# Copies of the rows of B and C in a state-space scan: two halves of 64 partitions that carry both, issued by SyncE

## The chip, the cores and the metric

One core of one Trainium2 chip. The time is the device time of one execution in microseconds (us), the median of several runs. The engines are TensorE (PE), VectorE (DVE), ScalarE (ACT), GpSimd (POOL) and SyncE (SP), with 16 DMA engines beside them. TensorE's clock has two levels, 1.2 and 2.4 GHz; the profile gives the granted clock as a mean, 1.00 being 2.4 GHz.

## The reference

Eight sequences of 512 tokens with 128 features go through four residual blocks, each after a layer norm: a state-space block, an FFN of 8 experts (all computed for all tokens, mixed by a softmax), a windowed attention of 16 heads, and the FFN again. The part that the change touches is the scan of the state-space block:

```python
b_term = jnp.tanh(b_raw)                       # [B, L, 8]
c_term = jnp.tanh(c_raw)                       # [B, L, 8]
decay = jnp.clip(jnp.exp(-delta[..., None] * a), 0.0001, 1.0)
drive = (1.0 - decay) * (b_term[:, :, None, :] * xb[..., None])
# over the tokens t, for 64 channels and 8 states:
state = dec_t * state + drv_t
y = jnp.sum(state * c_t[:, None, :], axis=-1) + D * x_t
```

b_term and c_term have one row for each of the 8 states, the same for all 64 channels.

## The kernel before

Features stand on the partitions and the 512 tokens in the free dimension. The time is laid out in chunks. A chunk is 128 of the 4096 hidden units of the FFN for one sequence: three fp32r matmuls of 512 columns for the gate and three for the up projection (weights and inputs are split in a high and a low part), SiLU on ScalarE (L1056), the product with the up projection on VectorE (L1094), and four down projections a little later (L1001). A pass has 32 chunks and there are 16 passes, so 512 chunks. The state-space block and the attention are woven in between: every engine has its own program, made by `interleave` (L938), which merges generators in the order of the slots that they yield. A slot is a time in chunks; it decides only the order of instructions on an engine, and the waits on semaphores decide when they run. The order on one engine is strict: behind a waiting instruction all others of this engine wait.

The scan of sequence i (i from 0 to 7) handles the 8 states in four steps k, two states at a time: partitions 0 to 63 are the 64 channels of state 2k, partitions 64 to 127 those of state 2k + 1. "State k" stands for such a step below. Sequence 0 is done ahead of the FFN with a spreading by TensorE. For sequences 1 to 7 `Ssm.spread` (L596) stores the 16 rows of B and C (`bc_rows`) in DRAM and reads them back spread: the two rows of B of step k, each to 64 partitions, go into `btile`, those of C into `ctile`. Both tiles are double, k % 2, and lie in `arena` at rows 6 and 7 (B) and 8 and 9 (C). The steps of a state, by line:

- ACT L493: exp, gives the decay. Waits for the y product of state k - 2.
- POOL L628: clips the decay. POOL L630: B times x (waits for the B copy).
- DVE L581 and L582: the drive, then the scan over 512 tokens.
- POOL L634: C times the state (waits for the C copy and the scan). POOL L638 adds it to y for k > 0; for k = 0 DVE L587 does.

The copy of B for state k waits for the scan of state k - 2 (L608), that of C for its y (L612). Both are issued by ScalarE, B at slot k - 2 and C at slot k + 0.5. The slots of the four states are 9, 12, 15, 18 for sequence 1 and 36, 39, 42, 45 for sequence 2; for sequences 3 to 7 they are o + 10, o + 16, o + 26, o + 32 with o = 64 (i - 2).

The attention of sequence j begins at slot 38 + 55j. On SP, `Att.sp` (L818) stores q and k to DRAM at +7 (L832), reads them back in another layout at +8 (L838: 8 copies of 256 KB), stores V at +9 (L845), and reads it back in windows at +12 and +20.2 (L860, 2 x 8 copies). POOL then makes masked queries (L883) and masked V (L891). SP also loads the inputs (L920), stores the outputs (L929) and reloads a residual buffer once the store has landed (L932, L933). The store of sequence b is at the end of its second FFN pass, two to four slots ahead of the first B copy of sequence b + 4.

The B copy before:

```python
act.dma_start(btile[k % 2], bc_r[2 * k:2 * k + 2, :].unsqueeze(1)
             .broadcast_to([2, INNER, L])).then_inc(b_moved[k % 2], 16)
```

Of the kernel before, what the change touches and what calls it, by code (L numbers as in the profile page):

```python
# [13 lines left out]
B, L, D = 8, 512, 128  # L14
P = 128
TT = L // P
INNER, DSTATE, DTRANK = 64, 8, 8
# [18 lines left out]
NC = NCH * NM  # L36
# [9 lines left out]
def _ssm_slots(i):  # L46
    if i == 0:
        return dict(ln=-33, win=-31, dt=-26, k=(-24, -23, -22, -21), y=-19)
    if i == 1:
        return dict(ln=1.5, win=3.5, dt=6, k=(9, 12, 15, 18), y=23.5)  # L50
    if i == 2:
        return dict(ln=26, win=28.5, dt=32, k=(36, 39, 42, 45), y=50.5)
    o = NCH * (2 * i - 4)
    return dict(ln=o + -9, win=o + -6.5, dt=o + 1, k=(o + 10, o + 16, o + 26, o + 32), y=o + 42)


T_SSM = [_ssm_slots(i) for i in range(B)]
T_ATT = [38 + 55 * b for b in range(B)]
ATT_PACE = [3.3] + [4.1] * (B - 2) + [3.22]

# [21 lines left out]
def build(nc, x_d, pack_d, wg_d, wu_d, wd_d, out_d):  # L82
    ctx = contextlib.ExitStack()
    with ctx:
# [3 lines left out]
        def sem(name):  # L88
            s = ctx.enter_context(nc.semaphore(name))
            sems.append(s)  # L90
            return s
# [41 lines left out]
        arena = sb("arena", [P, 10, L])  # L133
        xb2, zb, delta, tot, cv, sxT = (arena[:, i, :] for i in range(6))
        btile, ctile = ([arena[:, i + s, :] for s in range(2)] for i in (6, 8))
        bc_t = sb("bc_rows", [2 * DSTATE, L])
# [63 lines left out]
        bc_out = sem("bc_out")  # L200
        silu_x, xs_m, xs_done = sem("silu_x"), sem("xs_m"), sem("xs_done")
        dt_soft, delta_done = sem("dt_soft"), sem("delta_done")
        bx_done, dec_exp, scan_done = sem("bx_done"), sem("dec_exp"), sem("scan_done")
        dec_clip = sem("dec_clip")
        y_part, y_done, b_moved, c_moved = sem("y_part"), sem("y_done"), [sem("b_moved0"), sem("b_moved1")], [sem("c_moved0"), sem("c_moved1")]
        x_hi, qk_hi, qk_moved = sem("x_hi"), sem("qk_hi"), sem("qk_moved")
        qk_out = [[sem(f"{v}_{part}_out") for part in ("hi", "lo")] for v in "qk"]
        v_zero, v_pad, v_out, v_moved, p_t = sem("v_zero"), sem("v_pad"), sem("v_out"), [sem(f"v_moved{i}") for i in range(2)], sem("p_t")
# [57 lines left out]
        b = Banks(side_ps, side_full, side_free)  # L266
# [115 lines left out]
        class Ssm:  # L382
            @staticmethod
            def pe(pe, link, i):
                at = T_SSM[i]
                yield at["ln"]
# [206 lines left out]
                b.wait_free(dve, ("y", i))  # L593

            @staticmethod
            def spread(act, link, i):  # L596

                at = T_SSM[i]
                bc_r = bc_d[i % 2]
                yield at["dt"] + 1  # L600
                b.wait_free(act, ("bc", i))
                act.dma_start(bc_r, bc_t[:, :]).then_inc(bc_out, 16)
                for k in range(KT):
                    n = KT * i + k
                    yield at["k"][k] - 2
                    if k == 0:
                        act.wait_ge(bc_out, 16 * i)
                    act.wait_ge(scan_done, n - 1)  # L608
                    act.dma_start(btile[k % 2], bc_r[2 * k:2 * k + 2, :].unsqueeze(1)
                                 .broadcast_to([2, INNER, L])).then_inc(b_moved[k % 2], 16)  # L610
                    yield at["k"][k] + 0.5
                    act.wait_ge(y_done, n - 1)  # L612
                    act.dma_start(ctile[k % 2], bc_r[DSTATE + 2 * k:DSTATE + 2 * k + 2, :].unsqueeze(1)
                                 .broadcast_to([2, INNER, L])).then_inc(c_moved[k % 2], 16)

            @staticmethod
            def pool(pool, link, i):
                at = T_SSM[i]
                yield at["ln"] - 2
                norm_pool(pool, link, "ssm_ln", i)  # L620
                if i == 0:
                    return
                for k in range(KT):
                    n = KT * (i - 1) + k
                    d, bt, ct = dec[:, k % 2, :], btile[k % 2], ctile[k % 2]
                    yield at["k"][k] + 1.5
                    pool.wait_ge(dec_exp, KT * i + k + 1)
                    nc.gpsimd.tensor_scalar(d, d, 1e-4, 1.0, ALU.max, ALU.min).then_inc(dec_clip, 1)  # L628
                    pool.wait_ge(b_moved[k % 2], 16 * (n // 2 + 1))
                    nc.gpsimd.tensor_tensor(bt, bt, xb2, ALU.mult).then_inc(bx_done, 1)  # L630
                    yield at["k"][k] + 3.5
                    pool.wait_ge(c_moved[k % 2], 16 * (n // 2 + 1))
                    pool.wait_ge(scan_done, KT * i + k + 1)
                    nc.gpsimd.tensor_tensor(ct, ct, d, ALU.mult).then_inc(y_part, 1)  # L634
                    if k:
                        pool.wait_ge(y_part, n + 1)
                        pool.wait_ge(y_done, KT * i + k)
                        nc.gpsimd.tensor_tensor(tot, tot, ct, ALU.add).then_inc(y_done, 1)  # L638
# [299 lines left out]
        def interleave(jobs, eng, link, step):  # L938

            streams = []  # L940
            for program, k in jobs:
                gen = program(eng, link, k)
                streams.append([next(gen), gen])

            def run(c):
                while streams:
                    first = min(streams, key=lambda s: s[0])
                    if first[0] > c:
                        return
                    slot = next(first[1], None)  # L950
                    if slot is None:
                        streams.remove(first)
                    else:
                        first[0] = max(first[0], slot)

            for c in range(-SETUP, NC + LAG + 3):
                for _ in step(c) or ():
                    run(c)
                run(c + 0.5)
            run(10 ** 6)  # L960
# [6 lines left out]
        with nc.Block() as block:  # L967
# [47 lines left out]
            @block.sync  # L1015
            def _(sp):
                sp.dma_start(x_raw[:, :, :], tok(x_d, 0)).then_inc(raw_loaded, 16)
                sp.dma_start(pack[:, :], pack_d[:, NRAW:NPACK]).then_inc(packed, 16)
                sp.dma_start(raw, pack_d[:, 0:NRAW]).then_inc(raw_packed, 16)

                def chunk(c):
                    j = c + SETUP - 1
                    if 0 <= j < 2 * E:
                        if j >= NH:
                            sp.wait_ge(w_lo, j - NH + 1)
                        sp.dma_start(h_b[:, j % NH, :], (wg_d, wu_d)[j // E][j % E]).then_inc(w_loaded[j % NH], 16)
                    e = c + SETUP - 1 - 2 * E
                    if 0 <= e < E:
                        sp.dma_start(wd[:, CPE * e:CPE * (e + 1), :],
                                     wd_d[e].rearrange("(c p) h -> p c h", p=P)).then_inc(wd_loaded, 16)  # L1030

                interleave([(load_x, i) for i in range(B)] + [(store, i) for i in range(B)]
                           + [(pad_v, 0)] + [(Att.sp, j) for j in range(B)], sp, None, chunk)
                sp.wait_ge(stored, 16 * B)

            @block.scalar
            def _(act):
                link = Chain(act, act_step)

                def split_w(j):  # L1040
                    act.wait_ge(w_loaded[j % NH], 16 * (j // NH + 1))
                    nc.scalar.copy(w_part(j, 0), h_b[:, j % NH, :]).then_inc(w_hi, 1)

                def chunk(c):
                    if c < 0:
                        if 0 <= c + SETUP - 8 < 2 * E:
                            split_w(c + SETUP - 8)
                        return
                    if c < NC:
                        act.wait_ge(g_full, c + 1)  # L1050
                        if c == 0:
                            act.wait_ge(w_lo, 2 * E)
                            act.wait_ge(w_small, 2)
                        if c >= NH:
                            act.wait_ge(down_done, c - NH + 1)
                        nc.scalar.activation(h_b[:, c % NH, :], pg[c % 2][:, :], ACT.Silu).then_inc(gate_done, 1)  # L1056
                    yield

                def small_weights(act, link, k):
                    yield -SETUP  # L1060
                    act.wait_ge(w_prep, 1)
                    link(nc.scalar.activation(neg_a[:, :], neg_a[:, :], ACT.Exp, scale=-1.0))
                    nc.scalar.activation(neg_a[:, :], neg_a[:, :], ACT.Ln, bias=1.0).then_inc(w_prep, 1)

                interleave([(small_weights, 0)] + [(Ssm.act, i) for i in range(B)] + [(Ssm.spread, i) for i in range(1, B)] + [(Att.act, j) for j in range(B)]
                           + [(Head.act, m) for m in range(NM)], act, link, chunk)

            @block.vector
# [159 lines left out]
```

## Time and profile before

The runs had 1530.69 to 1531.13 us, median 1531.04. The profiled execution:

| | |
|---|---|
| time of the profiled execution | 1530.76 us |
| span | 1529.0 us |
| PE busy | 1442.1 us, 94% of the span |
| DVE busy | 946.7 us, 62% |
| ACT busy | 772.8 us, 51% |
| POOL busy | 503.1 us, 33% |
| ACT's queue (q10) | 14.91 MB, 2.7% of 16 engines |
| SP's queue (q1) | 58.58 MB, 14.7% of 16 engines |

Busy time of an engine is a sum over its instructions. A row of instructions gives the start, the duration, the engine, the line of the code, output and input by name, and in square brackets how long the engine was idle before it and what ended that. ACTq and SPq are issues of DMAs by the queues of these engines. "DMA share" is the mean busy share of the 16 DMA engines.

### The profile page before, as it was taken

To read this page: it belongs to the slowest core of one execution; us is meant where nothing else is said; L and a number is where in the kernel's file an instruction comes from. 1 tells how busy PE (TensorE), PEld (TensorE's weight loads), DVE (VectorE), ACT (ScalarE), POOL (GpSimd) and SP (SyncE) were. 2 spreads that over 40 slices of the span, in tenths; PEclk is the share of its full clock that TensorE was granted. 3 is DMA by queue.
4 is the path that set the end of the run, shared out by engine and by line. 5 is a ranking of instruction groups with operands and counts; after the bars stand their busy time and mean duration, and the time that the engine had idled before them with its cause. 6 is when DMAs were issued, how large, how long until landed. Compare 5 with 4: busy or idle time off the path is not lost.

```text
span 1529.0 us, 31357 instructions
## 1 busy us (share of the span) xinstructions
PE 1442.1 (94%) x12756; PEld 1247.8 (82%) x12756; DVE 946.7 (62%) x2125; ACT 772.8 (51%) x1037; POOL 503.1 (33%) x446
## 2 busy tenths in 40 slices
PE   5788889999999999999999989999999999999998
PEld 3677767888878878888888778888888888888887
DVE  5645558665766757666676566757765566575543
ACT  6453726654457444654546465455643554355321
POOL 5241344323432354135520373117511421241000
PEclk9999999999999999999999999999999999999999
DMA  5110151004201330024001510042004200420000
GB/s 184 33 48 23 45 143 32 19 27 131 40 2 41 105 81 2 9 89 116 14 2 39 134 43 13 1 136 57 29 2 118 40 2 1 118 40 1 2 7 8
DMA packets 82092, 75.50 MB, mean 49 GB/s; under 512 B 4748, under 2 KB 60076, under 8 KB 81948
## 3 DMA queue, kind: packets, MB, share of 16 engines
q1 hardware_dynamic: 74444, 58.58, 14.7%
q10 hardware_dynamic: 7504, 14.91, 2.7%
q8 instruction: 101, 1.65, 0.4%
q14 instruction: 43, 0.35, 0.1%
HBM read 60.65 MB, written 12.83 MB: 48 GB/s over the span
## 4 chain that ended last, share of the span: by engine, by line
PE 71%; DVE 9%; DMA 6%; ACT 5%; issue 5%; POOL 3%; SPq 1%; ACTq 0%; DVEq 0%; POOLq 0%
PE pd L1001 23%; PE pg L272 7%; PE pu L272 6%; PE pg L274 6%; PE pg L273 6%; PE pu L273 6%; PE pu L274 6%; DMA arena<-bc_spread 3%; PE att_ps L678 3%; DVE h L1094 2%; PE att_ps L700 2%; PE att_ps L705 1%; POOL arena L628 1%; DVE ffn_rows L295 1%; DMA qk_rows<-qk_parts 1%
## 5 line engine op out<-in xcount | busy, mean ns | idle before, releaser
L1056 ACT ACTIVATE h<-pg 128x512 f32<-128x512 f32 x512 | 303.4, 597 | 693.7 <-PE pg L274 687.5
L1001 PEld LDWEIGHTS pd<-w_down,h 128*128 128x128 f32 x4096 | 517.4, 194 | 31.9 <-issue 2.5
L1001 PE MATMUL pd<-w_down,h 128*128 128x128 f32 x4096 | 530.1, 278 | 0.8 <-DVE x L1082 0.8
L1094 DVE TENSOR_TENSOR h<-h,pu 128x512 f32<-128x512 f32 x512 | 345.6, 679 | 222.4 <-PE pu L274 220.7
L272 PE MATMUL pg<-ffn_x_hi,w_gate_hi 128*128 128x512 f32 x512 | 246.3, 481 | 1.5 <-DVE ffn_x_lo L355 1.5
L272 PE MATMUL pu<-ffn_x_hi,w_up_hi 128*128 128x512 f32 x512 | 207.0, 404 | 25.1 <-DVE h L1094 24.7
L273 PE MATMUL pg<-ffn_x_lo,w_gate_hi 128*128 128x512 f32 x512 | 204.6, 400 | 0.0
L274 PE MATMUL pg<-ffn_x_hi,w_gate_lo 128*128 128x512 f32 x512 | 204.4, 399 | 0.0
L273 PE MATMUL pu<-ffn_x_lo,w_up_hi 128*128 128x512 f32 x512 | 204.3, 399 | 0.0
L274 PE MATMUL pu<-ffn_x_hi,w_up_lo 128*128 128x512 f32 x512 | 204.2, 399 | 0.0
L903 POOL TENSOR_TENSOR att_arena<-att_arena 128x512 f32<-128x512 f32 (+1 forms) x72 | 72.8, 1011 | 349.4 <-DVE att_arena L775 349.2
L883 POOL TENSOR_TENSOR q_weights<-q,pack 128x512 fp32r<-128x512 f32 x136 | 140.8, 1056 | 79.9 <-DMA k<-qk_rows 79.9
L1056 ACT ACT_TABLE_LOAD x121 | 155.2, 1283 | 3.7 <-issue 1.6
L1082 DVE SCALAR_TENSOR_TENSOR x<-pd,mix,x 128x128 f32<-128x128 f32 x512 | 143.8, 344 | 20.3 <-PE pd L1001 14.8
L272 PEld LDWEIGHTS pu<-ffn_x_hi,w_up_hi 128*128 128x128 f32 x512 | 97.4, 190 | 57.4 <-DVE h L1094 34.6
L274 PEld LDWEIGHTS pg<-ffn_x_hi,w_gate_lo 128*128 128x128 f32 x512 | 97.7, 191 | 23.8
L274 PEld LDWEIGHTS pu<-ffn_x_hi,w_up_lo 128*128 128x128 f32 x512 | 97.2, 190 | 23.9
L273 PEld LDWEIGHTS pu<-ffn_x_lo,w_up_hi 128*128 128x128 f32 x512 | 97.5, 190 | 22.6
L272 PEld LDWEIGHTS pg<-ffn_x_hi,w_gate_hi 128*128 128x128 f32 x512 | 99.5, 194 | 9.9 <-issue 3.4
L273 PEld LDWEIGHTS pg<-ffn_x_lo,w_gate_hi 128*128 128x128 f32 x512 | 99.6, 195 | 5.0 <-issue 1.7
L628 POOL TENSOR_SCALAR arena<-arena 128x512 f32<-128x512 f32 x28 | 54.4, 1942 | 134.9 <-ACT arena L493 133.9
L733 ACT ACT_TABLE_LOAD x71 | 91.1, 1283 | 1.3
(192 smaller groups left out, 1539.2 us busy)
## 6 DMA issues: line engine op xcount, KB each, us to landing
arena<-bc_spread ACTq DMA_DIRECT2D x56, 256.0 KB
att_arena<-v_rows SPq DMA_DIRECT2D x64, 144.0 KB, 3.9
qk_rows<-qk_parts SPq DMA_DIRECT2D x32, 256.0 KB, 3.1
q<-qk_rows SPq DMA_DIRECT2D x32, 256.0 KB, 3.7
k<-qk_rows SPq DMA_DIRECT2D x32, 256.0 KB, 4.5
att_arena<-v_rows SPq DMA_DIRECT2D x64, 128.0 KB, 3.6
arena<-in_x SPq DMA_DIRECT2D x8, 256.0 KB, 2.8
x<-in_x SPq DMA_DIRECT2D x8, 256.0 KB, 3.5
```

Of the source, the lines that this page charges most:

```text
L272: nc.tensor.matmul(out, w[0], x_parts[0], start=first, stop=False)
L273: nc.tensor.matmul(out, w[0], x_parts[1], start=False, stop=False)
L274: return nc.tensor.matmul(out, w[1], x_parts[0], start=False, stop=last)
L628: nc.gpsimd.tensor_scalar(d, d, 1e-4, 1.0, ALU.max, ALU.min).then_inc(dec_clip, 1)
L678: last = nc.tensor.matmul(ps[:, (4 * i + g) * WK:(4 * i + g + 1) * WK], q_w[:, n % 2, i, g, :, :].rearrange("p r q -> p (r q)"), k3[:, g, ...
L733: nc.scalar.activation(u, u, ACT.Exp, scale=float(HD) ** -0.5).then_inc(s_exp, 1)
L883: nc.gpsimd.tensor_tensor(q_w[:, n % 2, i, :, :, :], q3[:, :, w * WQ:w * WQ + QW].bitcast(F32).unsqueeze(2) .broadcast_to([P, 4, 4, QW]), ...
L903: nc.gpsimd.tensor_tensor(u, u, smax[:, 0:nw, :].unsqueeze(3).broadcast_to([P, nw, 4, WK]), ALU.subtract).then_inc(s_sub, 1)
L1001: last = nc.tensor.matmul(pd[:, t * P:(t + 1) * P], h_b[:, d % NH, t * P:(t + 1) * P], wd[:, d % NCH, :], start=d % CPE == 0 and t == 0, s ...
L1056: nc.scalar.activation(h_b[:, c % NH, :], pg[c % 2][:, :], ACT.Silu).then_inc(gate_done, 1)
L1082: nc.vector.scalar_tensor_tensor(x[:, t, :], pd[:, t * P:(t + 1) * P], mix[m % 2][:, t, e % E:e % E + 1], x[:, t, :], ALU.mult, ALU.add).t ...
L1094: nc.vector.tensor_tensor(h, h, pu[d % 2][:, :], ALU.mult).then_inc(h_done, 1)
```

## The change

One copy carries, for one half h of the partitions, the B row and the C row of state 2k + h: it writes 64 partitions x 2 rows x 512, from two rows of DRAM that lie 8 apart. Two such copies, h = 0 and 1, make a state. They are issued together, by SP instead of ScalarE, at the slot `bc`, and wait for the scan and for the y of state k - 2. The `bc` slot is k - 2 or, where that is later, 5.5 slots behind the slot of state k - 2: 7, 10, 14.5, 17.5 in sequence 1; 34, 37, 41.5, 44.5 in sequence 2; k - 2 from sequence 3 on. The store of the 16 rows moves to SP too. POOL waits for both copies in front of L630 and no longer in front of L634.

```diff
--- before.py
+++ after.py
@@ -55,6 +55,9 @@
 
 
 T_SSM = [_ssm_slots(i) for i in range(B)]
+for t in T_SSM:
+
+    t["bc"] = [max(k - 2, t["k"][n - 2] + 5.5 if n >= 2 else -NC) for n, k in enumerate(t["k"])]
 T_ATT = [38 + 55 * b for b in range(B)]
 ATT_PACE = [3.3] + [4.1] * (B - 2) + [3.22]
 
@@ -202,7 +205,7 @@
         dt_soft, delta_done = sem("dt_soft"), sem("delta_done")
         bx_done, dec_exp, scan_done = sem("bx_done"), sem("dec_exp"), sem("scan_done")
         dec_clip = sem("dec_clip")
-        y_part, y_done, b_moved, c_moved = sem("y_part"), sem("y_done"), [sem("b_moved0"), sem("b_moved1")], [sem("c_moved0"), sem("c_moved1")]
+        y_part, y_done, bc_moved = sem("y_part"), sem("y_done"), [sem("bc_moved0"), sem("bc_moved1")]
         x_hi, qk_hi, qk_moved = sem("x_hi"), sem("qk_hi"), sem("qk_moved")
         qk_out = [[sem(f"{v}_{part}_out") for part in ("hi", "lo")] for v in "qk"]
         v_zero, v_pad, v_out, v_moved, p_t = sem("v_zero"), sem("v_pad"), sem("v_out"), [sem(f"v_moved{i}") for i in range(2)], sem("p_t")
@@ -593,25 +596,25 @@
                 b.wait_free(dve, ("y", i))
 
             @staticmethod
-            def spread(act, link, i):
+            def spread(sp, link, i):
 
                 at = T_SSM[i]
                 bc_r = bc_d[i % 2]
                 yield at["dt"] + 1
-                b.wait_free(act, ("bc", i))
-                act.dma_start(bc_r, bc_t[:, :]).then_inc(bc_out, 16)
+                b.wait_free(sp, ("bc", i))
+                sp.dma_start(bc_r, bc_t[:, :]).then_inc(bc_out, 16)
                 for k in range(KT):
                     n = KT * i + k
-                    yield at["k"][k] - 2
+                    yield at["bc"][k]
                     if k == 0:
-                        act.wait_ge(bc_out, 16 * i)
-                    act.wait_ge(scan_done, n - 1)
-                    act.dma_start(btile[k % 2], bc_r[2 * k:2 * k + 2, :].unsqueeze(1)
-                                 .broadcast_to([2, INNER, L])).then_inc(b_moved[k % 2], 16)
-                    yield at["k"][k] + 0.5
-                    act.wait_ge(y_done, n - 1)
-                    act.dma_start(ctile[k % 2], bc_r[DSTATE + 2 * k:DSTATE + 2 * k + 2, :].unsqueeze(1)
-                                 .broadcast_to([2, INNER, L])).then_inc(c_moved[k % 2], 16)
+                        sp.wait_ge(bc_out, 16 * i)
+                    sp.wait_ge(scan_done, n - 1)
+                    sp.wait_ge(y_done, n - 1)
+
+                    for h in range(2):
+                        sp.dma_start(arena[h * INNER:(h + 1) * INNER, 6 + k % 2:10:2, :],
+                                      bc_r[2 * k + h::DSTATE, :].unsqueeze(0)
+                                      .broadcast_to([INNER, 2, L])).then_inc(bc_moved[k % 2], 16)
 
             @staticmethod
             def pool(pool, link, i):
@@ -626,10 +629,9 @@
                     yield at["k"][k] + 1.5
                     pool.wait_ge(dec_exp, KT * i + k + 1)
                     nc.gpsimd.tensor_scalar(d, d, 1e-4, 1.0, ALU.max, ALU.min).then_inc(dec_clip, 1)
-                    pool.wait_ge(b_moved[k % 2], 16 * (n // 2 + 1))
+                    pool.wait_ge(bc_moved[k % 2], 32 * (n // 2 + 1))
                     nc.gpsimd.tensor_tensor(bt, bt, xb2, ALU.mult).then_inc(bx_done, 1)
                     yield at["k"][k] + 3.5
-                    pool.wait_ge(c_moved[k % 2], 16 * (n // 2 + 1))
                     pool.wait_ge(scan_done, KT * i + k + 1)
                     nc.gpsimd.tensor_tensor(ct, ct, d, ALU.mult).then_inc(y_part, 1)
                     if k:
@@ -1030,7 +1032,7 @@
                                      wd_d[e].rearrange("(c p) h -> p c h", p=P)).then_inc(wd_loaded, 16)
 
                 interleave([(load_x, i) for i in range(B)] + [(store, i) for i in range(B)]
-                           + [(pad_v, 0)] + [(Att.sp, j) for j in range(B)], sp, None, chunk)
+                           + [(pad_v, 0)] + [(Ssm.spread, i) for i in range(1, B)] + [(Att.sp, j) for j in range(B)], sp, None, chunk)
                 sp.wait_ge(stored, 16 * B)
 
             @block.scalar
@@ -1062,7 +1064,7 @@
                     link(nc.scalar.activation(neg_a[:, :], neg_a[:, :], ACT.Exp, scale=-1.0))
                     nc.scalar.activation(neg_a[:, :], neg_a[:, :], ACT.Ln, bias=1.0).then_inc(w_prep, 1)
 
-                interleave([(small_weights, 0)] + [(Ssm.act, i) for i in range(B)] + [(Ssm.spread, i) for i in range(1, B)] + [(Att.act, j) for j in range(B)]
+                interleave([(small_weights, 0)] + [(Ssm.act, i) for i in range(B)] + [(Att.act, j) for j in range(B)]
                            + [(Head.act, m) for m in range(NM)], act, link, chunk)
 
             @block.vector
```

## Rows read from the trace of the kernel before

**Rows 1.** The chain that ended last, by engine, whole span.

```profile
PE 71%; DVE 9%; DMA 6%; ACT 5%; issue 5%; POOL 3%; SPq 1%; ACTq 0%; DVEq 0%; POOLq 0%
```

**Rows 2.** Groups of instructions, 1440 to 1500 us: busy, mean ns, idle before.

```profile
L1056 ACT ACTIVATE h<-pg 128x512 f32<-128x512 f32 x26 | 15.5, 598 | 42.1 <-PE pg L274 42.1
```

**Rows 3.** Windows: length, busy time by engine, granted clock, DMA share, GB/s.

```profile
core 0: us, PE busy (x) PEld busy (x) DVE busy (x) ACT busy (x) POOL busy (x), PEclk, DMA share, GB/s
100.00:110.00 10.00, 8.02 (x41) 6.67 (x40) 4.02 (x8) 5.03 (x6) 5.75 (x4) 0.84 0.13 49
200.00:210.00 10.00, 6.11 (x29) 4.47 (x28) 5.26 (x9) 1.79 (x3) 2.93 (x3) 0.94 0.65 209
850.00:890.00 40.00, 32.19 (x235) 28.16 (x234) 18.18 (x32) 13.48 (x17) 18.72 (x15) 0.83 0.47 109
1030.00:1070.00 40.00, 38.57 (x413) 33.08 (x412) 28.13 (x48) 21.84 (x28) 29.05 (x21) 0.96 0.26 60
```

**Rows 4.** Waits, whole span: total us, times, longest.

```profile
POOL arena L634 <- DMA arena<-bc_spread: 48.0, 11, 7.8
...
POOL arena L630 <- DMA arena<-bc_spread: 9.8, 8, 2.9
```

**Rows 5.** Timeline of POOL, states of sequences 1 and 2.

```profile
81.88 1.93 POOL L628 TENSOR_SCALAR arena<-arena 128x512 f32<-128x512 f32 x1 [25.10 <-ACT arena L493]
84.39 1.29 POOL L630 TENSOR_TENSOR arena<-arena 128x512 f32<-128x512 f32 x1 [0.59 <-DMA arena<-bc_spread]
...
105.79 1.27 POOL L630 TENSOR_TENSOR arena<-arena 128x512 f32<-128x512 f32 x1 [0.72 <-DMA arena<-bc_spread]
111.14 1.27 POOL L634 TENSOR_TENSOR arena<-arena 128x512 f32<-128x512 f32 x1 [4.08 <-DMA arena<-bc_spread]
112.49 1.28 POOL L638 TENSOR_TENSOR arena<-arena 128x512 f32<-128x512 f32 x1
113.85 1.92 POOL L628 TENSOR_SCALAR arena<-arena 128x512 f32<-128x512 f32 x1
116.48 1.26 POOL L630 TENSOR_TENSOR arena<-arena 128x512 f32<-128x512 f32 x1 [0.71 <-DMA arena<-bc_spread]
...
178.49 1.28 POOL L630 TENSOR_TENSOR arena<-arena 128x512 f32<-128x512 f32 x1 [2.01 <-DMA arena<-bc_spread]
```

**Rows 6.** DMA issues, whole span: count, KB each, median us to landing.

```profile
q<-qk_rows SPq DMA_DIRECT2D x32, 256.0 KB, 3.7
...
arena<-in_x SPq DMA_DIRECT2D x8, 256.0 KB, 2.8
```

**Rows 7.** Timeline of VectorE: a scan of sequence 1, then the L581 of sequence 2.

```profile
107.17 0.69 DVE L581 SCALAR_TENSOR_TENSOR arena<-arena 128x512 f32<-128x512 f32 x1 [5.94 <-POOL arena L630]
107.90 1.22 DVE L582 TENSOR_TENSOR_SCAN arena<-arena 128x512 f32<-128x512 f32 x1
...
179.88 0.69 DVE L581 SCALAR_TENSOR_TENSOR arena<-arena 128x512 f32<-128x512 f32 x1 [2.61 <-POOL arena L630]
...
191.24 0.69 DVE L581 SCALAR_TENSOR_TENSOR arena<-arena 128x512 f32<-128x512 f32 x1 [5.62 <-POOL arena L630]
...
204.70 1.66 DVE L581 SCALAR_TENSOR_TENSOR arena<-arena 128x512 f32<-128x512 f32 x1 [4.84 <-POOL arena L630]
```

**Rows 8.** Timeline of ScalarE's queue: the first B copy, and one in sequence 2.

```profile
76.81 1.08 ACTq L609 DMA_DIRECT2D arena<-bc_spread  x1
...
181.87 4.50 ACTq L609 DMA_DIRECT2D arena<-bc_spread  x1
```

**Rows 9.** The chain of waits at sequence 6's states: start, length.

```profile
837.78 7.01 DMA qk_rows<-qk_parts
...
849.33 10.65 DMA k<-qk_rows
```

**Rows 10.** Timeline of POOL in sequence 4's last state and sequence 6's states.

```profile
536.81 2.04 POOL L883 TENSOR_TENSOR q_weights<-q,pack 128x512 fp32r<-128x512 f32 x2 [6.31 <-DMA k<-qk_rows]
...
541.59 1.27 POOL L630 TENSOR_TENSOR arena<-arena 128x512 f32<-128x512 f32 x1 [0.73 <-DMA arena<-bc_spread]
...
860.05 4.03 POOL L883 TENSOR_TENSOR q_weights<-q,pack 128x512 fp32r<-128x512 f32 x4 [3.25 <-DMA k<-qk_rows]
...
877.50 1.89 POOL L891 TENSOR_TENSOR att_arena<-att_arena,pack 128x1024 f32<-128x1024 f32 x1 [9.07 <-DMA att_arena<-v_rows]
```

## The prediction

> **What bounds the kernel now.** Read the engine shares first. TensorE is busy for most of the span and holds most of the chain that ended last; DMA has only 6% of that chain [rows 1]. In the last stretch, where nothing runs beside the FFN, 26 SiLU evictions take 60 us, so a chunk costs 2.31 us [rows 2]: that is TensorE's own pace. What can be gained is the time in which TensorE falls off it, so the next view is the windows. In the stretches where the state updates of sequences 1 and 2 run, PE is busy 8.02 and 6.11 of 10 us at a granted clock of 0.84 and 0.94; where those of sequence 6 run, 32.19 of 40 us at 0.83 [rows 3]. These are the late places, and in each the line of waits leads to the copies of B and C. POOL waited 48.0 us in 11 waits at L634 and 9.8 us in 8 at L630 for them [rows 4]. (A wait goes to what came last, so part of the 4.08 us in front of an L634 is VectorE's scan.)
>
> Why the copies are late is in the window of sequence 1: nothing else moves there, the DMA share is 0.13 and the rate 49 GB/s [rows 3]. 0.13 is 2 of 16 engines (0.125). B and C each write [2, 64, 512]: two state rows, each repeated 64 times, with the 2 outermost. The pace agrees: the multiplications L630 of two consecutive states, each released by its B copy, start at 105.79 and 116.48 [rows 5], and between two B copies lies one C copy, so 512 KB take 10.69 us, 5.35 us a copy.
>
> A rule of the Trainium skill ("DMA: Bandwidth & Descriptors", section "Rules for kernel authors") says that the outermost dimension's size caps the number of DMA engines, a small leading broadcast included. For a before-copy that gives 2, and this trace agrees (0.13); for the new copies, with 64 outermost, it gives 16, which no row here shows for this shape. The sum below needs only that a pair lands within 7 us.
>
> **What the change does.** (a) 56 copies of 256 KB stay 56 copies of 256 KB, but each carries B and C for 64 partitions, 64 outermost. Their landing isn't in the trace of before. Nearest rows: other 256 KB copies whose outermost size is 32 or 128 land in a median of 3.7 us (in a queue of four) and 2.8 us [rows 6]; the old form needs 10.7 us for two. I take 4 us a pair: 2.8 us, plus 0.5 us for the second issue (the issue cost of 0.5 us is that of the old ones, and stays two a state), plus 0.7 us for its bytes (5.35 us x 2 of 16 engines). Ends: 3 us and 10.7 us.
>
> (b) The state chain of sequence 1. A step is L628, L630 on POOL, L581 and L582 on VectorE, L634, L638 on POOL. Its bare length: L628 1.92, L630 1.27, VectorE from 107.17 to 109.12 = 1.95, L634 1.27, L638 1.28, and five hand-overs of about 0.1: 8.2 us [rows 5, 7]. It now runs at 10.69, the pace of the DMA. The slots leave 3 chunks a step, 6.9 us at 2.31, so TensorE stays bound by the chain, through the multiplication L1094 queued behind L581 on VectorE, both before and after. Three steps between the first L581 and the last save 3 x 2.5 = 7.5 us, and the 0.59 us that the first L630 waited [rows 5] go too: **8 us**.
>
> (c) Sequence 2. VectorE was idle 2.61, 5.62 and 4.84 us before the L581 of states 1, 2 and 3 [rows 7], so it was ready at 177.3, 185.6 and 199.9. State 1: L630 at 178.49 had waited 2.01 for B [rows 5], so L581 comes at 177.9, ready and released, instead of 179.88. State 2: one bare step later, 186.1, after VectorE's 185.6, instead of 191.24. State 3: before, VectorE got ready 8.6 us after the L581 of state 2, more than a bare step (8.2): 186.1 + 8.6 = 194.7 instead of 204.70. **10 us.** In this stretch ScalarE's own queue also stood behind an issue of 4.50 us [rows 8]; that stall goes as well, inside the same 10 us.
>
> (d) Sequence 6 collides with the attention of sequence 4, whose q and k go to DRAM and back on all 16 engines, two of which are still full of B and C. The last of four stores lands 7.01 us after issue, the last k copy 10.65 us after its own [rows 9], where the medians were near 3.7 [rows 6]; POOL's queries start only at 860.05 and its first V mask at 877.50 after 9.07 us of wait [rows 10]. PE is idle 7.8 of the 40 us from 850, and a clock of 0.83 means a third of them at the lower level (1.2 instead of 2.4 GHz), 6.8 us of full-speed work: some 13 us in all, where the two overlap a little. Sequence 7's states, 1030 to 1070, have the same work and an attention beside it, and lose 1.4 + 1.6 = 3.0 us [rows 3]. With the copies spread, a pair adds 128 x 2 / 16 = 16 packets to an engine, some 1.4 us, instead of 10.7 us to two. I take **8 us** of the 10 between them.
>
> (e) Sequence 4, state 3: POOL's L883 waited 6.31 us for k and L630 another 0.73 for B [rows 10]. L630 can start about 2.5 us earlier with TensorE idle behind it: **2.5 us**. For sequences 3, 5 and 7 I count nothing: B lands before POOL gets there.
>
> (f) Issues leave ScalarE: 63 at about 0.5 us, 31 us. They lie under table loads and waits for TensorE; worth 0, bound 0 to 3 us. On SP they cost nothing of themselves, but SP runs in order: behind a waiting pair stand the q/k stores (sequence 2: slots 44.5 and 45), the V reads (sequences 5 and 7), and before pair 0 of sequences 4 to 7 the store of a result and the reload that waits for it, some 4 us. The pair is issued 3.5 slots (8 us) before L630 wants it and takes 4, so this is worth 0, bound 0 to -4 us.
>
> (g) The new wait: B now waits for y of the state two before, not only its scan. That is L587 or L638, which end a whole bare step or nearly (8 to 10 us) before L630 wants the pair; 4 us fit. Cost 0, up to a pair of 8 us.
>
> **Sum.** 8 + 10 + 8 + 2.5 = 28.5 us. The profiled execution took 1530.76 us (span 1529.0); less 28.5 is 1502.3, and the median of the runs lies 0.3 higher: 1502.6, say **1503**. Bounds: all of (d) and 3 us of (f), -37 us; or (d) at nothing, (c) at 7 us and (e) at 2, -17 us.
>
> **The rivals.**
> 1. Half comes back. The attention start of sequence 6 is late by POOL's order, not by DMA: between 864 and 884 POOL also has masks, queries and states, and in sequence 2 the q/k/V round trip then ends last. For: at 860.05 stands L883 x4, a POOL job of 4.03 us, before the next L628. Against: each of these jobs is preceded by a DMA wait [rows 10]. Then 8 + 7 + 0 + 2 = 17 us: 1514.
> 2. More than counted: with less idling the clock stays at its upper level, and the sequence 6 stretch comes back whole. 37 us: 1494.
> 3. Slower. The copies stay narrow, on two engines or as slow by reading the same two rows 16 times at once. A pair then takes 10.7 us and POOL can't begin L630 before C is in too, where it now needs B alone: 5.35 us later at state 0 of sequences 1 and 2, the pace of 10.7 unchanged after it. Plus 11 us: 1542. It decides from a pair time of about 7 us (issue 76.81 [rows 8] to the end of L628 at 83.8 [rows 5]). For: every engine would read the same 4 KB, which no row shows. Against: one engine reads one 2 KB row 64 times over now without a visible penalty.
> 4. It does nothing measurable, since TensorE makes up the lateness elsewhere. Against: it can't run faster than 2.31 us a chunk [rows 2], and in most windows it does so already.
>
> One more rule of the Trainium skill speaks against the cut ("SBUF — State Buffer", section "Can I just issue two DMAs to hit both halves?"): a copy of 64 partitions reaches only half of the SBUF's ports, and two such copies run one behind the other. An estimate by its 196 GB/s for 64 partitions is 1.3 us a copy, a pair in about 5 us with a fixed cost of 2; no row here shows a 64-partition copy. By it the sum stays, with 2 us of slack instead of 3, and rival 3 gets nearer.
>
> **Chances.** Forecast 0.60, rival 1 0.22, rival 2 0.08, rival 3 0.06, rival 4 0.04. A difference under 0.2% (3 us) can't be told from none. Faster 0.90, same 0.04, slower 0.06. Range 1492 to 1518: it holds the forecast, rival 2 and rival 1 with its spread.
>
> **What would show it.** In the windows of sequence 1's states the DMA share stands in bursts well over 0.13, and L630 has no DMA wait. The L630 starts of sequence 1 lie 8.2 us apart, not 10.7. The POOL waits on B and C fall from 58 us to under 5. The k copies of sequence 6's time land in under 6 us and queries start before 855. SP shows new waits on L587 or L638, with nothing urgent behind them. Wrong: copies still at 5 us each; a step still over 10 us; or TensorE's idle time moved to another wait of the same length.

## The result and the profile after

The changed kernel takes 1492.66 us (median of 4 runs, 1490.37 to 1494.68) against 1530.87 us: a ratio of 0.9754, 95% interval 0.9739 to 0.9768, 38 us faster. (The 1530.87 us are the median of the runs above with one more, of 1529.60.) The range, from 1492 us, held the median by 0.7 us, and two of the four runs lie below it; the forecast of 1503 us was 10 us too high. Runs in a slower state of the chip (two of the first four of the width-only kernel below, 2548 and 2817 us, and one of the narrow kernel's four, 1627 us) are in none of the times and ratios here. The profiled execution took 1493.85 us, with a span of 1492.1 us.

The chain that ended last (from the page of the profile), by engine, and the DMA row of the new copies: DMA has 1% of it where it had 6% [rows 1].

```profile
PE 77%; DVE 10%; ACT 5%; issue 5%; POOL 4%; DMA 1%; DVEq 0%; SPq 0%; POOLq 0%; ACTq 0%
...
arena<-bc_spread SPq DMA_DIRECT2D x56, 256.0 KB, 4.8
```

The timeline of POOL in sequence 1 (start, duration; L631, L633, L636 and L640 are L628, L630, L634 and L638 of before):

```profile
82.54 1.93 POOL L631 TENSOR_SCALAR arena<-arena 128x512 f32<-128x512 f32 x1 [24.82 <-ACT arena L496]
84.55 1.28 POOL L633 TENSOR_TENSOR arena<-arena 128x512 f32<-128x512 f32 x1
...
100.47 1.28 POOL L633 TENSOR_TENSOR arena<-arena 128x512 f32<-128x512 f32 x1
103.89 1.29 POOL L636 TENSOR_TENSOR arena<-arena 128x512 f32<-128x512 f32 x1 [2.14 <-DVE arena L585]
105.26 1.27 POOL L640 TENSOR_TENSOR arena<-arena 128x512 f32<-128x512 f32 x1
106.62 1.91 POOL L631 TENSOR_SCALAR arena<-arena 128x512 f32<-128x512 f32 x1
108.61 1.27 POOL L633 TENSOR_TENSOR arena<-arena 128x512 f32<-128x512 f32 x1
```

See two things. Two L633 of consecutive states start 8.14 us apart (100.47, 108.61), where it was 10.69 [rows 5]; and no line has a wait for DMA; nor has any POOL instruction a wait for B or C in the whole span, where these waits were 57.8 us [rows 4]. In front of L636 only the scan is left, 2.14 us where 4.08 stood.

Windows, with the columns of [rows 3]: two short ones in sequence 1, and 40 us of sequence 6's states, which now come some 24 us earlier (the window is moved by 22).

```profile
78.00:80.00 2.00, 1.97 (x9) 1.31 (x8) 1.58 (x5) 1.42 (x4) 0.00 (x0) 1.00 0.68 223
...
100.00:110.00 10.00, 9.41 (x58) 7.96 (x57) 4.91 (x10) 5.68 (x7) 7.42 (x6) 1.00 0.19 53
...
828.00:868.00 40.00, 39.02 (x366) 33.88 (x364) 28.83 (x58) 23.98 (x30) 27.96 (x23) 1.00 0.42 83
```

The copies come in bursts (223 GB/s at a DMA share of 0.68, so at least 11 of the 16 engines) instead of a steady 49. PE is busy 9.41 us of the ten (8.02 before), and in sequence 6 39.02 of 40 at a clock of 1.00 (32.19 at 0.83 before, [rows 3]).

Where the time went is read most simply from one instruction that stands in both kernels 512 times, the SiLU of a chunk (L1056 before, L1058 after). Its start in the two profiled executions, from the trace, us:

```
chunk                  0      8     24     40     56    160    168    272    280    344    352    504
before               56.1   78.0  127.5  175.5  232.6  534.1  558.8  856.7  892.1 1073.5 1100.2 1501.2
after                57.0   78.7  119.6  167.8  212.9  514.1  534.9  832.9  856.8 1036.7 1063.3 1464.3
earlier by           -1.0   -0.7    7.9    7.8   19.8   20.0   24.0   23.8   35.4   36.9   36.9   36.9
```

All of it is gained in five short places, and between them the two executions run in step: 8.6 us at sequence 1's states (chunks 8 to 24), 12.0 at sequence 2's (40 to 56), 4.0 at sequence 4's last state (160 to 168), 11.6 where sequence 6 meets attention 4 (272 to 280), 1.5 in sequence 7 (344 to 352). The start is 1 us later. (One execution of each kernel is profiled, so a place is known to about 1 us.)

SP's queue has the new waits for y (L590 and L640 are L587 and L638 of before; waits of the queue: total, times, longest), and behind them nothing that was late: POOL's waits for k fell from 79.9 to 71.3 us in all, and its 9.1 us for V are gone.

```profile
SPq L612 <- DVE arena L590: 86.0, 5, 32.5
...
SPq L612 <- POOL arena L640: 33.3, 4, 13.6
```

### The profile page after: what moved, and what is told of

The parts are those of the page before. It is cut to its first block, busy times and chain, and to the rows that moved or that the text cites. A ratio compares the mean times of both kernels' runs of the same rounds, so it can differ in the third digit from the quotient of the medians.

```text
span 1492.1 us, 31350 instructions
## 1 busy us (share of the span) xinstructions
PE 1427.2 (96%) x12756; PEld 1236.2 (83%) x12756; DVE 950.3 (64%) x2125; ACT 773.0 (52%) x1037; POOL 504.3 (34%) x446
## 4 chain that ended last, share of the span: by engine, by line
PE 77%; DVE 10%; ACT 5%; issue 5%; POOL 4%; DMA 1%; DVEq 0%; SPq 0%; POOLq 0%; ACTq 0%
PE pd L1003 25%; PE pg L275 7%; PE pu L275 7%; PE pg L277 6%; PE pu L276 6%; PE pg L276 6%; PE pu L277 6%; PE att_ps L680 3%; DVE h L1096 2%; PE att_ps L702 2%; POOL arena L631 1%; PE att_ps L707 1%; DVE ffn_rows L298 1%; POOL arena L633 1%; DVE x L1084 1%
## 5 line engine op out<-in xcount | busy, mean ns | idle before, releaser
L1058 ACT ACTIVATE h<-pg 128x512 f32<-128x512 f32 x512 | 303.5, 597 | 658.3 <-PE pg L277 655.2
L1003 PEld LDWEIGHTS pd<-w_down,h 128*128 128x128 f32 x4096 | 512.2, 192 | 31.8 <-issue 2.7
L885 POOL TENSOR_TENSOR q_weights<-q,pack 128x512 fp32r<-128x512 f32 x136 | 141.3, 1060 | 71.3 <-DMA k<-qk_rows 71.3
L631 POOL TENSOR_SCALAR arena<-arena 128x512 f32<-128x512 f32 x28 | 53.8, 1921 | 142.0 <-ACT arena L496 141.3
```

Of the source, the lines that this page charges most:

```text
L885: nc.gpsimd.tensor_tensor(q_w[:, n % 2, i, :, :, :], q3[:, :, w * WQ:w * WQ + QW].bitcast(F32).unsqueeze(2) .broadcast_to([P, 4, 4, QW]), ...
L1003: last = nc.tensor.matmul(pd[:, t * P:(t + 1) * P], h_b[:, d % NH, t * P:(t + 1) * P], wd[:, d % NCH, :], start=d % CPE == 0 and t == 0, s ...
```

## The experiments

**The issuing queue alone.** The changed kernel with its copies issued by ScalarE:

```diff
-interleave(... + [(Ssm.spread, i) for i in range(1, B)] + [(Att.sp, j) for j in range(B)], sp, ...
+interleave(... + [(Att.sp, j) for j in range(B)], sp, ...
-interleave([(small_weights, 0)] + [(Ssm.act, i) ...] + [(Att.act, j) ...
+interleave([(small_weights, 0)] + [(Ssm.act, i) ...] + [(Ssm.spread, i) for i in range(1, B)] + [(Att.act, j) ...
```

> The changed kernel, with the same two wide copies a state at the same slots and behind the same waits, but issued by ScalarE's queue as before. Width theory (the gain comes from the copies using 16 DMA engines instead of 2): the whole gain stays, 1490 to 1498 us; a few us may go where ScalarE stands behind the wait for y. Queue theory (the gain comes from taking the issues off ScalarE): most of the 38 us is lost, 1520 us or more.

Measured: 1494.7 us, ratio to before 0.9765 (0.9748 to 0.9783), the same as the changed kernel within both intervals. With wide copies the queue makes no difference that these runs can tell.

**The width alone.** The kernel before, with each copy cut into two of 64 partitions:

```diff
-act.dma_start(btile[k % 2], bc_r[2 * k:2 * k + 2, :].unsqueeze(1)
-             .broadcast_to([2, INNER, L])).then_inc(b_moved[k % 2], 16)
+for h in range(2):
+    act.dma_start(btile[k % 2][h * INNER:(h + 1) * INNER, :], bc_r[2 * k + h:2 * k + h + 1, :]
+                  .broadcast_to([INNER, L])).then_inc(b_moved[k % 2], 16)
...
```

The same is done for C, and POOL waits for both halves.

> The kernel before with one thing changed: each copy of B and of C is cut into two of 64 partitions with 64 outermost (4 copies of 128 KB a state). ScalarE issues them at the old slots, B waits for the scan alone, C for y. Width theory: nearly the whole gain, 1490 to 1500 us, DMA share in bursts far above 0.13 in the states of sequence 1 and steps of 8.2 us. Theory of grouping or of the queue: 1515 us or more.

Measured: ratio 0.9757 (0.9734 to 0.9779), 1492.46 and 1494.12 us. Two further runs of the same kernel, for its profile:

> The same kernel as e4_wide_only (old slots, old waits, ScalarE's queue, 4 copies of 64 partitions a state) once more, for a profile at the full clock. 1490 to 1496 us; steps of 8.1 to 8.3 us in sequence 1, the POOL waits on B and C under 3 us in all, and the time at chunk 64 within 1.5 us of the changed kernel's.

Measured: 1495.16 us, ratio 0.9771 (0.9725 to 0.9817). The timeline of POOL, two steps of sequence 1 (L633 is L630):

```profile
100.19 1.29 POOL L633 TENSOR_TENSOR arena<-arena 128x512 f32<-128x512 f32 x1
...
108.41 1.27 POOL L633 TENSOR_TENSOR arena<-arena 128x512 f32<-128x512 f32 x1
```

8.22 us a step, no wait for DMA. Width alone makes the gain; neither the move to SP nor the pairing of B and C is needed for it. By the chunk times it comes at the same places: 8.4 us at sequence 1, 11.7 at sequence 2, 4.0 at sequence 4, 11.6 between chunks 272 and 280. There the queries of attention 4 (L886 is L883) wait for nothing, where they had waited 3.25 us for k [rows 10]:

```profile
828.92 4.49 POOL L886 TENSOR_TENSOR q_weights<-q,pack 128x512 fp32r<-128x512 f32 x4
```

**Everything but the width.** The changed kernel with one copy of B and one of C for 128 partitions, 2 outermost:

```diff
-for h in range(2):
-    sp.dma_start(arena[h * INNER:(h + 1) * INNER, 6 + k % 2:10:2, :],
-                  bc_r[2 * k + h::DSTATE, :].unsqueeze(0).broadcast_to([INNER, 2, L])).then_inc(bc_moved[k % 2], 16)
+for row, tile in ((2 * k, btile[k % 2]), (DSTATE + 2 * k, ctile[k % 2])):
+    sp.dma_start(tile, bc_r[row:row + 2, :].unsqueeze(1).broadcast_to([2, INNER, L])).then_inc(bc_moved[k % 2], 16)
```

> The changed kernel with its SP queue, its slots and its waits, but each pair is one copy of B and one of C for 128 partitions with 2 outermost, as before. Rival 3 of the prediction: slower than before, 1542 us (5.3 us later at state 0 of sequences 1 and 2). If pairing and the wait for y cost nothing: 1531 us. Queue theory: well below 1531 us, 1510 or less.

Measured: 1548.62 us, ratio 1.0114 (1.0091 to 1.0138), slower than before. POOL in sequence 1 (L632 is L630):

```profile
89.16 1.26 POOL L632 TENSOR_TENSOR arena<-arena 128x512 f32<-128x512 f32 x1 [5.29 <-DMA arena<-bc_spread]
...
99.84 1.29 POOL L632 TENSOR_TENSOR arena<-arena 128x512 f32<-128x512 f32 x1 [4.01 <-DMA arena<-bc_spread]
```

The first pair is 5.29 us late, as rival 3 had it (5.35), and the steps keep 10.7 us. The whole is 18 us slower, not 11: by the chunk times sequences 1 and 2 lose 8 us, not 11, and sequences 4, 5 and 7, which the rival had left out, some 3, 4 and 5; the stretch of sequence 6 gives 1.5 back.

**The old copies on SP.** The kernel before with `Ssm.spread` moved to SP, slots and waits unchanged.

> The kernel before with its copies, slots and waits, issued by SP instead of ScalarE. Width theory: 1528 to 1534 us, since DMA still paces the states at 10.7 us and ScalarE's issue time lay under waits for TensorE. Queue theory: a clear gain, 1515 us or less. Slower than 1534 us if SP's order (q and k behind waiting copies) costs.

Measured: 1523.83 us, ratio 0.9957 (0.9942 to 0.9972): 7 us faster, between the two theories. By the chunk times it is 4.0 us behind before at chunk 56, level with it at 168 and 272, and 7.1 us ahead at 280: what it gains in all, it gains at chunks 272 to 280. There SP's timeline is

```profile
837.80 2.08 SPq L832 DMA_DIRECT2D qk_rows<-qk_parts  x4
839.93 2.60 SPq L838 DMA_DIRECT2D q<-qk_rows  x4
842.57 2.54 SPq L838 DMA_DIRECT2D k<-qk_rows  x4
845.16 0.53 SPq L613 DMA_DIRECT2D arena<-bc_spread  x1
```

The first q read waits for the first of the four stores. It starts at 839.93, so that store had landed after 2.1 us; in the kernel before it took 7.01 us [rows 9]. The narrow copy of B came 7.3 us ahead of the stores here (issued at 830.49), and 2.1 us ahead of them in the kernel before (835.68). The narrow copy of C is issued after the q and k copies, and POOL waits 6.05 us for it, until 855.05; the queries follow at once, with no wait for k. So with narrow copies the moments of issue decide who waits, and with wide ones nobody waits for them (first two experiments).

**Sequence 6 alone narrow**, by a condition `if i == 6` between the two forms of the diff above.

> The changed kernel, with the copies of sequence 6 alone cut as before (2 outermost: one copy of B, one of C). Term (d) theory, that the 11.6 us gained where sequence 6's states meet attention 4 come from q, k and V no longer standing behind B and C on two engines: 6 to 11 us slower than the changed kernel (1499 to 1504 us), all of it lost between chunks 264 and 288, the rest of the run as in the changed kernel. Rival 1 (POOL's own order makes that start late): 1494 us, no loss.

Measured: 1502.99 us, ratio 0.9818 (0.9788 to 0.9848), 10 us more than the changed kernel. By the chunk times it gains 2.3 us between chunks 272 and 280 (from 25.5 us ahead of before to 27.8), where the changed kernel gains 11.6, and it loses another 1.6 by chunk 290, at the last state of the sequence; elsewhere the two agree within 1 us. Timeline of POOL (L638 is L630, L890 is L883):

```profile
829.76 4.04 POOL L890 TENSOR_TENSOR q_weights<-q,pack 128x512 fp32r<-128x512 f32 x4 [2.81 <-DMA k<-qk_rows]
833.99 1.92 POOL L636 TENSOR_SCALAR arena<-arena 128x512 f32<-128x512 f32 x1 [0.18 <-ACT arena L496]
842.19 1.26 POOL L638 TENSOR_TENSOR arena<-arena 128x512 f32<-128x512 f32 x1 [6.29 <-DMA arena<-bc_spread]
```

The loss of 10 us that term (d) had put down to the narrow copies is there, and rival 1, which had none, falls. The path is only in part that of the kernel before. The four stores again land late, 7.5 to 7.9 us after their issue (2.0 to 2.7 in the changed kernel), and POOL waits 2.81 us for k; but the longest wait, 6.29 us, is for the pair of state 1; the kernel before has no wait in front of that L630 (866.16). The clearest evidence for (d) is the width-only kernel, in which POOL has the order and the waits of before: it gains the whole 11.6 us.

**Sequences 1 and 2 alone narrow.**

> The changed kernel, with the copies of sequences 1 and 2 alone cut as before. Terms (b) and (c), and the loss that the all-narrow kernel showed up to chunk 64 (28 us against the changed kernel): 1519 to 1523 us, steps of 10.7 us in sequence 1, and nothing lost after chunk 64. If the two terms overlap with later ones (time made up or given back later): under 1512 us.

Measured: 1521.68 us, ratio 0.9934 (0.9916 to 0.9953), 29 us more than the changed kernel. At chunk 64 it is 9.7 us behind before, the changed kernel 19.8 ahead; the later gains come as in the changed kernel (-4.7 at 272, 6.8 at 280). Nothing is made up later: the places add.

**A dose: 4 engines.** Four copies of 128 KB a state, each with 4 outermost:

```diff
+for row, tile in ((2 * k, btile[k % 2]), (DSTATE + 2 * k, ctile[k % 2])):
+    for h in range(2):
+        sp.dma_start(tile[h * INNER:(h + 1) * INNER, :], bc_r[row + h:row + h + 1, :].unsqueeze(1)
+                     .broadcast_to([4, INNER // 4, L])).then_inc(bc_moved[k % 2], 16)
```

> The changed kernel with a dose: four copies of 128 KB a state (B and C, each half), issued together on SP, with 4 outermost, so 4 engines. Bytes take 5.35 x 2 / 2 = 5.35 us a pair, about 8 us with issue and landing. The prediction said that it decides from about 7 us at state 0 and 8.2 us a step: 1 to 2 us late at state 0 of sequences 1 and 2, the steps still 8.2 to 8.5 us: 1494 to 1501 us. If the gain were in proportion to the width it would be near 1512.

Measured: 1498.74 us, ratio 0.9794 (0.9762 to 0.9826). Waits, whole span:

```profile
POOL arena L633 <- DMA arena<-bc_spread: 4.5, 4, 2.1
```

The first L633 of sequence 1 waits 0.61 us, no more. In the window 78 to 80 us the DMA share is 0.24, 4 of 16. Two engines to four bring 50 us (1548.6 to 1498.7), four to sixteen some 6. From the first issue to the L633 that it releases, the first pair takes 8.6 us here (75.36 to 83.93), 13.3 on two engines (75.91 to 89.16), and in the changed kernel it lands after 5.3. So the gain is not in proportion: most of it is had once a pair takes about as long as a bare step, 8.2 us. Where between two and four engines it sets in was not measured.

**Steps further apart.** The changed kernel with other slots: k=(8.5, 12, 15.5, 19) for sequence 1 and k=(35, 38.5, 42.5, 46) for sequence 2.

> The changed kernel with the states of sequences 1 and 2 further apart: slots 8.5, 12, 15.5, 19 and 35, 38.5, 42.5, 46, 3.5 chunks a step instead of 3. The chain of a step is 8.2 us and 3 chunks are 6.9 us, 3.5 are 8.1. If TensorE still loses the difference at each step: 3 to 6 us faster than the changed kernel, 1487 to 1491 us. If other work fills these steps already (q, k, V and layer norms beside them): no change, 1492 to 1495 us. Slower if the last state comes too late for y at slots 23.5 and 50.5.

Measured: 1492.32 us, ratio 0.9749 (0.9721 to 0.9777), no difference to the changed kernel. In the 40 us from 80 PE is busy 39.17 us here and 38.43 in the changed kernel; what the slots could still give there is below 1 us.

**What slows a wide copy.** A pair had been put at 4 us; a single copy lands after 4.8. Two kernels in which the copies read rows of the input x instead of B and C, which changes what the scan computes: first 128 different rows for the same 64 partitions, then the same with one tile of 128 partitions a copy.

```diff
-                  bc_r[2 * k + h::DSTATE, :].unsqueeze(0).broadcast_to([INNER, 2, L])
+                  x_d[i - 1:i + 1].rearrange("b (p t) d -> p b (t d)", p=P)[h * INNER:(h + 1) * INNER]
```

> The changed kernel, but the two copies of a state read 128 different rows of 2 KB (rows of the input x, which stand in for B and C: the result is not the reference's) and not two rows 64 times over. Same shape on the SBUF's side: 64 partitions a copy, 128 packets of 2 KB. In the changed kernel a copy lands 4.8 us (median) after its issue, where 4 us had been taken for a pair. If reading the same two rows by 16 engines at once is what slows them: the median falls to 3 to 3.5 us. If it is the 64 partitions: it stays at 4.5 to 5 us. Time of the kernel either way 1490 to 1496 us.

> As the one before (rows of x stand in for B and C), but each copy writes one tile of 128 partitions (256 KB, 128 outermost) instead of two tiles of 64. If 64 partitions are what slows a copy: the median to landing falls to about 3 us, and the rate at the start of sequence 1 rises over 300 GB/s. If the rows read were the cause, no difference to the kernel before this. Time of the kernel 1490 to 1496 us.

Measured: 1493.82 and 1493.0 us, no difference to the changed kernel. Landing of the 56 copies (L615) of the changed kernel, then with 128 different rows for 64 partitions, then with 128 partitions:

```profile
DMA to landing us min/median/max: 3.9/4.8/7.0
```

```profile
DMA to landing us min/median/max: 3.4/4.4/6.6
```

```profile
DMA to landing us min/median/max: 2.5/3.5/6.5
```

And the window of the first burst, in which all three move the first two pairs (4 copies, 1 MB), in the same order:

```profile
77.50:83.00 5.50, 5.47 (x32) 4.50 (x31) 2.77 (x7) 4.87 (x7) 0.46 (x1) 1.00 0.72 194
```

```profile
77.50:83.00 5.50, 5.47 (x32) 4.47 (x31) 2.58 (x7) 4.87 (x7) 0.64 (x1) 1.00 0.75 194
```

```profile
77.00:81.00 4.00, 3.96 (x23) 3.12 (x22) 2.73 (x7) 3.41 (x5) 0.00 (x0) 1.00 0.85 260
```

The full 128 partitions take 0.9 us off a copy, and the rate over the burst goes from 194 to 260 GB/s. Other rows to read take off 0.4 us and leave the rate as it is; even the 0.4 us may be something else, since the copies of the first experiment, which read the same two rows, land in a median of 4.4 us too. So it is mostly the shape of 64 partitions (the outermost size changes with it, from 64 to 128; the two are not told apart). The rule of the Trainium skill that was weighed ("SBUF — State Buffer", section "Can I just issue two DMAs to hit both halves?") points the same way: only a transfer of all 128 partitions reaches all the ports. That the two halves run strictly one behind the other is not shown: in the second of the three kernels the window from 80 to 82 us has 286 GB/s. The difference costs nothing here, since the slack of a step covers it.

## Why the prediction was right, and where its sizes were off

- What bounds the kernel: right. B and C on 2 of 16 engines paced the state steps, and the width-only kernel shows it by itself. The rule of the Trainium skill on the outermost dimension ("DMA: Bandwidth & Descriptors", "Rules for kernel authors") holds for the new shape as far as the traces tell: a share of 0.68 can't come from two engines, and a size of 4 gives 0.24 and a time in between.
- (a) The first pair takes 5.3 us (the second issue comes 0.7 us after the first and lands 4.5 us later), not 4. The bound that mattered, 7 us at state 0, was kept: L633 does not wait. "Copies still at 5 us each" had been named as a sign of being wrong, and the median of a copy is 4.8 us; the sign was badly chosen, since two narrow copies ran one behind the other (10.7 us a pair) and two wide ones overlap.
- (b) 8.6 us measured, 8 forecast: steps of 8.14 us against 8.2.
- (c) 12.0 against 10. The L581 of states 1 to 3 of sequence 2 stand at 170.28, 178.44 and 186.58 in the changed kernel. With the 7.8 us of sequence 1 taken off, those of before [rows 7] would be 172.1, 183.4 and 196.9, so they are earlier by 1.8, 5.0 and 10.3 us; the working had 2.0, 5.1 and 10.0. The other 1.7 us come behind the last state, where POOL had waited 7.77 us for C and nothing was counted.
- (d) 11.6 against 8: the largest miss. The mechanism held: the queries start at 828.55 (852.4 on the clock of before; 855 was asked for), and the q and k copies land within 6.0 us. I had read 13 us of loss, kept 3 as sequence 7's [rows 3] suggested, and taken 8 of the 10 from caution. PE is now busy 39.02 of 40 at full clock: the loss went nearly whole, clock included. Two readings were off without use in the sum: the store of 7.01 us was the first of the four (all four took 6.9 to 7.3), and the median of 3.7 us is that of q alone; k's was 4.5.
- (e) 4.0 against 2.5: POOL's wait for k goes from 6.31 to 0.70 us, and its L630 has none.
- Nothing was counted for sequence 7, which gained 1.5 us. No wait made it. From 1062 to 1066 us of the kernel before TensorE was busy throughout at a granted clock of 0.57, and its matmuls of 512 columns took 0.63 us; the same work of the changed kernel ran at 1.00, in 0.40 us each. Both kernels had kept TensorE busy for 2.6 of the 4 us before; why the clock fell in the one alone is not shown.

```profile
1062.00:1066.00 4.00, 4.00 (x71) 2.96 (x72) 3.16 (x8) 0.60 (x1) 4.00 (x5) 0.57 0.00 2
```

```profile
1026.00:1030.00 4.00, 4.00 (x86) 3.37 (x85) 4.00 (x10) 0.60 (x1) 3.92 (x5) 1.00 0.14 48
```

- The same is part of every place of the gain. In the kernel before the granted clock fell to means of 0.57 to 0.72 in the stretches 100 to 104, 110 to 114, 194 to 200, 208 to 212, 546 to 550, 860 to 868 and 880 to 888 us; in the changed kernel it stands at 1.00 in all five places. Term (d) counted this; (b), (c) and (e) got their sizes from the chain alone.
- (f), (g) Right at zero: SP's new waits hold nothing up, moving the issue back to ScalarE changes nothing, and the width-only kernel, without the new wait for y, is no faster.
- Rivals: 1 is refuted by the width-only kernel and the narrow sequence 6. 2, with a chance of 0.08, came 1.3 us from the result (1494), where the forecast, with 0.60, missed by 10; and it did so for its reason: the clock stays at its upper level, and the stretch comes back whole. 3 has the right mechanism, shown by the kernel with everything but the width, but was priced 7 us too low: its 11 us for sequences 1 and 2 were 8, and sequences 4, 5 and 7, some 12 us together, stood at nothing. 4 is out.

So the mechanism was right, and the size a quarter too small: 28.5 us forecast, 38 measured. That the range still held the median, by 0.7 us, is luck as much as working. What was missed is 3.6 us at (d), held back from caution, 2.0 and 1.5 us beyond the terms of sequences 2 and 4, and the 1.5 us of sequence 7. The traces show the places to be separate and additive.

## What to carry to other kernels

When a window shows a DMA share of 2/16 or 4/16 with nothing else on the queues, look at the outermost dimension of the copy before its bytes or its queue: here the same bytes cut otherwise were worth 2.4%. Price a faster transfer by the chain that it frees (its bare step length), and expect little more once it fits into that step. Where TensorE idles at such a place, look at the granted clock there too. Look also for transfers of other work that share the few engines: 11.6 of the 38 us were gained in an attention that the change never touched.

## What the runs showed of the hardware beyond that

Copies on 2 engines also hold up copies on 16 engines that are issued soon behind them. In the kernel before, a narrow B copy is issued at 835.68 and four stores of 256 KB from 837.78; they land after 6.9 to 7.3 us. In the width-only kernel, with the same queues, the same order and the same 2.1 us between (812.16 and 814.26), they land after 2.9 to 3.2 us. It is not a matter of two queues: with sequence 6 narrow and all copies on SP's queue (B and C from 805.61, the stores from 812.31) they take 7.5 to 7.9 us, and with the old copies on SP, where B is issued 7.3 us ahead, 2.0 to 2.6. Wide copies of 64 partitions each moved 194 GB/s over a burst of four, those of 128 partitions 260.
